# Router logits with the router's weights stationary and the tokens streaming, and an order of steps written for that

## The reference, cut to what matters

```
logits = einsum('th,eh->te', x, gate_weight)      # 512 tokens x 32 experts
probs = softmax(logits)
top_val, top_idx = top_k(probs, 8);  top_val = top_val / sum(top_val)
w_tg = top_val summed into 8 groups by merge_groups[top_idx]
h = einsum('th,goh->tgo', x, gate_up_proj[dominant_experts])
gate, up = split(h);  act = silu(gate) * up
out = einsum('tg,tgh->th', w_tg, einsum('tgi,ghi->tgh', act, down))
```

## Time and profile before

| | us |
|---|---|
| median of three runs | 1121.26 |
| lowest, highest | 1115.88, 1122.84 |
| the profiled execution | 1118.26 |
| its span, first to last instruction | 1116.2 |
| one element in the loop (the copy L906 of one element to that of the next, 302.07 to 432.10) | 130.03 |
| TensorE busy over the span | 1019.5 |
| VectorE busy over the span | 755.6 |
| ScalarE busy over the span | 400.0 |
| GpSimd busy over the span | 420.0 |

### The profile page before, as it was taken

One profiled execution on the slowest core, in us unless ns is written; L12 is line 12 of the kernel. 1 busy time (PEld: TensorE's weight loads), 2 busy tenths in 40 slices (PEclk: granted clock), 3 DMA queues, 4 the chain that ended last, 5 costly groups with the idle time before them and its releaser, 6 DMA issues.

```text
span 1116.2 us, 24959 instructions
## 1 busy us (share of the span) xinstructions
PE 1019.5 (91%) x9856; PEld 739.1 (66%) x9856; DVE 755.6 (68%) x1516; ACT 400.0 (36%) x715; POOL 420.0 (38%) x349
## 2 busy tenths in 40 slices
PE   6979989999999999999899999999999998998768
PEld 4556667766776667766676667766677666776456
DVE  6767677675867767586776858577675777757335
ACT  4335432254214533154322542144331553224210
POOL 1627333364316333273333643154332733326100
PEclk9989999999999999999999999999999999999879
DMA  6220000200011000200002000010002000010000
GB/s 187 57 86 2 1 1 1 68 2 2 1 27 43 2 1 1 68 2 1 1 1 69 1 2 1 10 59 2 2 1 68 2 2 1 1 49 2 2 0 19
DMA packets 22232, 23.59 MB, mean 21 GB/s; under 512 B 6314, under 2 KB 20138, under 8 KB 22130
## 3 DMA queue, kind: packets, MB, share of 16 engines
q1 hardware_dynamic: 22130, 22.02, 6.5%
HBM read 17.80 MB, written 4.21 MB: 20 GB/s over the span
## 4 chain that ended last, share of the span: by engine, by line
PE 82%; DVE 9%; issue 4%; ACT 3%; POOL 1%; DMA 1%; DVEq 0%; POOLq 0%; ACTq 0%; SPq 0%
PE ring L1119 17%; PE ring L976 13%; PE ring L977 10%; PE ring L978 10%; PE ring L1190 8%; PE av L1135 6%; PE ring L1099 6%; DVE mcol L858 3%; PE ring L1090 2%; PE ring L1037 2%; PE ring L1107 1%; PE ring L1179 1%; PE av L1148 1%; ACT pt L670 1%; ACT xn L629 1%
## 5 line engine op out<-in xcount | busy, mean ns | idle before, releaser
L670 ACT ACTIVATE pt<-ring 128x384 f32<-128x384 f32 (+1 forms) x384 | 171.0, 533 | 357.5 <-PE ring L1119 315.0
L858 DVE TENSOR_REDUCE mcol<-ring 128x1 f32<-128x128 f32 (+3 forms) x512 | 212.0, 481 | 51.5 <-PE ring L1099 49.5
L560 POOL TENSOR_SCALAR_AFFINE_SELECT pt<-pt 128x512 f32<-128x512 f32 x128 | 83.2, 662 | 345.2 <-ACT pt L670 345.2
L834 DVE TENSOR_TENSOR prod<-ring,table 128x1024 f32<-128x1024 f32 x128 | 156.2, 1221 | 81.4 <-PE ring L978 59.2
L1119 PE MATMUL ring<-rows 32*128 32x512 f32 (+3 forms) x3072 | 165.2, 329 | 25.9 <-DVE mcol L858 15.7
L551 POOL TENSOR_TENSOR rows<-prod,rows 128x1024 fp32r<-128x1024 f32 x64 | 152.4, 2385 | 86.9 <-ACT rows L650 86.9
L1119 PEld LDWEIGHTS ring<-rows 32*128 32x128 f32 x3072 | 118.9, 185 | 74.8 <-issue 41.3
L544 POOL TENSOR_TENSOR prod<-prod 128x512 f32<-128x512 f32 x64 | 84.7, 1324 | 112.3 <-DVE prod L834 112.1
L976 PE MATMUL ring<-h_hi,gu_lo 128*128 128x512 f32 x192 | 80.7, 420 | 14.2 <-DVE h_lo L819 14.2
L1135 PE MATMUL av<-pt,vals 128*17 128x512 f32 (+3 forms) x1024 | 83.7, 440 | 10.1 <-POOL pt L560 10.1
L976 PE MATMUL ring<-h_hi,wq_lo 128*128 128x512 f32 x192 | 84.1, 438 | 1.8 <-DVE wq_lo L780 1.5
(11 more groups left out here) (159 smaller groups left out, 1651.4 us busy)
## 6 DMA issues: line engine op xcount, KB each, us to landing
xn<-x_dram SPq DMA_DIRECT2D x8, 512.0 KB, 4.3
xr<-x_dram SPq DMA_DIRECT2D x8, 512.0 KB, 3.7
out_dram<-xr SPq DMA_DIRECT2D x8, 512.0 KB, 3.2
gate_bc<-gates_scratch SPq DMA_DIRECT2D x8, 256.0 KB, 5.0
pt<-wmod_dram SPq DMA_DIRECT2D x1, 1536.0 KB, 6.4
pt<-gup_t_dram SPq DMA_DIRECT2D x16, 96.0 KB, 2.6
dn<-wu_t_dram SPq DMA_DIRECT2D x1, 640.0 KB, 9.8
xr<-wk_t_dram SPq DMA_DIRECT2D x1, 512.0 KB, 7.9
```

The costliest lines, as they stand in the source:

```text
L670: sc.activation(pt[:, PT_AT[n] + h * w:PT_AT[n] + (h + 1) * w], ps[:, 0:w], ACT.Exp, scale=SCALE).then_inc(exp_ready.sem, 1)
L834: ve.tensor_tensor(prod[:, s % PROD, :, :], ps[:, :].unsqueeze(1).broadcast_to([P, 2, S]), table[:, :, :], ALU.mult).then_inc(rotated.sem, 1)
L858: last = ve.reduce_max(mcol[:, q, h * HR + HD:h * HR + HD + 1], ps[:, at:at + (q + 1) * P], AX_X)
```

## The change

It does three things. First, the logits are computed with the router's 32 columns of weights as the stationary operand and all 512 tokens streaming, six matmuls, so that the output stands as experts by tokens in 32 partitions of the same ring bank. Second, this has to be turned back: ScalarE copies the 32 partitions to SBUF (`logits_copy`), TensorE transposes four blocks into `av` (`turn_l`), and VectorE copies from there (`turned_l`) in the place of `logits_out`. The values of the next element, which also use `av`, wait for that copy. Third, both texts of the order are written anew; the setup's is as it was. The body's text has 252 steps for 250.

```diff
-                "logits": lambda: (logits_read, ahead, 0),
+                "logits": lambda: (logits_copied, ahead, 0),
...
+                    elif kind == "logits_copy":
+                        ps = wait_full(sc, b, part, ("logits", ahead))
+                        sc.activation(lgT, ps[0:NX, :], ACT.Copy).then_inc(logits_copied.sem, 1)
...
-                    elif kind == "logits_out":
-                        ps = wait_full(ve, b, part, ("logits", ahead))
-                        ve.tensor_copy(lg, ps[:, 0:TT * NX].rearrange("p (t n) -> p t n", t=TT)).then_inc(logits_read.sem, 1)
+                    elif kind == "turned_l":
+                        wait(ve, logits_turned, b, ahead, 0)
+                        ve.tensor_copy(lg, av[:, 0:TT * NX].rearrange("p (t n) -> p t n", t=TT)).then_inc(logits_read.sem, 1)
...
-                                wait(pe, mix_gated, b, ahead - 1, 0)
+                                wait(pe, logits_read, b, ahead - 1, 0)
...
                     elif kind == "logits":
                         ps = take_bank(pe, b, part, step)
+                        three(ps[0:NX, :], *columns(gw_hi, gw_lo, 0, NX), *rows2,
+                              ready=lambda c: wait(pe, lo_ready[1], b, ahead, c)).then_inc(full_sem, 1)
+                    elif kind == "turn_l":
+                        wait_alone(pe, logits_copied, b, ahead, 0)
+                        wait_alone(pe, mix_gated, b, ahead, 0)
                         for t in range(TT):
-                            tok = t * P
-                            last = three(ps[:, t * NX:(t + 1) * NX],
-                                         lambda c: h2_hi[:, c, tok:tok + P], lambda c: h2_lo[:, c, tok:tok + P],
-                                         lambda c: gw_hi[:, c, :], lambda c: gw_lo[:, c, :],
-                                         ready=lambda c: wait(pe, lo_ready[1], b, ahead, c) if t == 0 else None)
-                        last.then_inc(full_sem, 1)
+                            last = pe.transpose(av[:, t * NX:(t + 1) * NX], lgT[:, t * P:(t + 1) * P], ident[0:NX, 0:NX])
+                        last.then_inc(logits_turned.sem, 1)
```

Two lines of the body's text, as an example of the third part (the end of the attention, then the router):

```diff
-combine.101 qcon.10 exp.031 score.032 qcon_hi.10 value.030 qcon_lo.10 hi.101 exp.032 clear.031 lo.100 value.031
+score.031 clear.030 value.030 exp.031 score.032 clear.031 rope.1010 exp.032 clear.032 rope.1011 value.031 value.032
```

More of the change, by code:

```diff
@@ L103 @@
-weighed.00 weighed.01 weigh.04 weigh.05 upped.05 weighed.02 weighed.03 hi.111 weighed.04 weighed.05 down.00 lo.110
-kcon_hi.11 kcon_lo.11 join.00 down.01 join.01 lo.111 store.0
+load_next.1 loads.0 maxima.010 rope.0200 reduce.010 score.000 rotate.0200 rope.0201 exp.000 rotate.0201 maxima.011
+rope.0210 clear.000 reduce.011 score.001 rope.0211 exp.001 rotate.0210 combine.020 clear.001 maxima.012 rotate.0211
+combine.021 value.000 value.001 reduce.012 score.002 hi.020 shift.01 qcon.02 lo.020 exp.002 kcon.02 qcon_hi.02
@@ new lines @@
+modulate1.11 low1.10 score.020 exp.020 score.021 low1.11 clear.020 exp.021 attn_out.01 clear.021 rope.1000
+maxima.031 rotate.1000 value.020 reduce.031 maxima.032 reduce.032 value.021 score.022 exp.022 shift.03 shifted.03
+rope.1001 score.030 clear.022 value.022 rotate.1001 exp.030 attn_out.02 latent.1 latent_hi.1 latent_lo.1 combine.100
+score.031 clear.030 value.030 exp.031 score.032 clear.031 rope.1010 exp.032 clear.032 rope.1011 value.031 value.032
+hi.100 lo.100 rotate.1010 rotate.1011 kcon.10 kcon_hi.10 attn_out.03 values.10 rope.1100 combine.101 hi.101 mix.00
@@ new lines @@
+mix.01 values.11 rotate.1100 kcon_lo.10 qcon.10 mixed.00 mixed.01 values_out.10 qcon_hi.10 lo.101 qcon_lo.10
+maxima.100 stats2.0 reduce.100 values_out.11 maxima.101 rope.1101 rope.1110 pow2.0 norm2.0 turn2.00 reduce.101
+turn2.01 rotate.1101 modulate2.00 rope.1111 modulate2.01 qcon.11 qcon_hi.11 rotate.1110 combine.110 low2.00
+maxima.102 low2.01 logits.0 rotate.1111 logits_copy.0 qcon_lo.11 gate.00 hi.110 combine.111 turn_l.0 lo.110
+reduce.102 turned_l.0 tanh.00 hi.111 gate.01 tanh.01 gate.02 tanh.02 gated.00 up.00 up.01 top.0 shift.10 gate.03
@@ L119 @@
[L119 to L123 removed]
+loads.0 maxima.010 rope.0200 reduce.010 score.000 rotate.0200 rope.0201 exp.000 rotate.0201 maxima.011 rope.0210
@@ new lines @@
+clear.000 reduce.011 score.001 rope.0211 exp.001 rotate.0210 combine.020 clear.001 maxima.012 rotate.0211
+combine.021 value.000 value.001 reduce.012 score.002 hi.020 shift.01 qcon.02 lo.020 exp.002 kcon.02 qcon_hi.02
+clear.002 rope.0300 shifted.01 hi.021 qcon_lo.02 kcon_hi.02 score.010 rotate.0300 value.002 exp.010 rope.0301
+kcon_lo.02 score.011 attn_out.00 lo.021 rope.0310 rotate.0301 exp.011 maxima.020 clear.010 value.010 rotate.0310
+combine.030 reduce.020 score.012 exp.012 rope.0311 maxima.021 qcon.03 rotate.0311 reduce.021 maxima.022 combine.031
```

56 lines of the change are left out of this document (21 added, 35 removed).

## The result

The changed kernel took 1101.43 us in the median of four runs (1100.39 to 1104.50), the kernel before 1119.99 beside it; the ratio is 0.9842, with a 95% interval from 0.9803 to 0.9880. The forecast of 1093 was 8 us too low, and the time lies just beyond the forecast's own range (1084 to 1100); the range for 8 in 10, 1084 to 1110, held it because that takes in the rival *half filled* as well.

What follows compares the result with a forecast made beforehand. TensorE was taken to bound the kernel, busy 1019.5 of 1116.2 us. Net 2.9 us of waits plus 0.6 for the router, 3.5 times 7, plus 1.7 gave 26.2 us less: 1093 us, range for 8 in 10 1084 to 1110.

Steps and rivals of the forecast that it cites:

- half filled: Rival, chance 0.18: the two larger new waits come out twice as long as VectorE's queue slips; 11 us more, 1104.
- The router's work: Router logits on TensorE: 2.68 - 1.40 - 0.36 - 0.3 for changes of form, 0.6 us less per element.
- the two figures cited there: The Trainium skill's matmul prices: about 25 ns start to start for short ones, 215.7 ns for 512 columns.
- The filled waits: Five TensorE waits per loop element, 0.88, 0.62, 1.06, 1.14 and 1.49, filled by the new order: together 5.19 us.
- cover of 2.4 us against 2.2: Ahead of `mix.00`: `kcon.10`, `values.10` and `rope.1100` take 2.4 us on TensorE and cover `attn_out.03`, 2.2 us.
- The new waits: Waits the new order makes: 0.8 at `maxima.030`, 0.8 at `maxima.100`, 0.7 for smaller ones; 2.3 us per element.
- 0.7 together, between 0 and 1.5: Smaller new waits per element: `maxima.101` for a bank of `maxima.100`, and `gate.00` for a bank read by `rotate.1111`.
- The clock: Granted clock in the loop, 1.00 in the profile before; its fall under 1.00 was named only as a sign of error.
- two of the signs named there: Signs of a wrong forecast: an element over 128.5 us, and the loop's granted clock under 1.00.
- The last element: Element without a next one: 2.5 us of waits filled, router 0.6, less 0.8 and 0.6; sum 1.7 us.
- GpSimd's queue: Rival *slower*, chance 0.06: late GpSimd work makes TensorE wait at `value.002` and `value.011`, 5.85 us per element, 1133.
- the covers of 0.8 and 0.4: Slack in us expected before TensorE would wait on GpSimd at `value.002` (0.8) and `value.011` (0.4); cost nothing.

Runs made afterwards that it cites:

- e9: The changed kernel with six matmuls whose result nobody reads put between `maxima.100` and `maxima.101`; 1096.76 us.
- e5: The kernel of e3, but GpSimd's `lo.101` waits for the second residual addition on VectorE instead of the first; 1085.40 us.
- e6: The kernel of e5 with `rope.1101` put ahead of `maxima.101` on TensorE and `rotate.1101` ahead of `reduce.101` on VectorE; 1082.36 us.
- e3: The changed kernel with two GpSimd waits more: `combine.101` until `attn_out.03` has multiplied, `lo.101` until the first residual addition is done; 1089.56 us.
- e12: The order and two GpSimd waits of e6 with the old router of 24 short matmuls; 1099.29 us.
- e1: The changed kernel's new order of steps with the old router of 24 short matmuls; 1118.14 us, ratio 0.9988 to the kernel before.
- e10: The kernel of e1 with six matmuls whose result nobody reads put between `maxima.100` and `maxima.101`; 1120.74 us.
- e2: The kernel before, in its old order of steps, with the new router; 1106.30 us, ratio 0.9888 to the kernel before.
- e8: The kernel of e2 with GpSimd's `lo.100` moved behind `clear.032` and held so that it runs beside the multiplication of `attn_out.03`; 1133.06 us.

## Why the prediction was right, and which step failed

- **The router's work**, 0.6 us per element: 0.75 measured (1.40 for six matmuls, 0.36 for the transposes). The 0.3 for changes of form was too much; the rest of the term held. `turn_l` waits for nothing. (By the two figures cited there the total would be some 16 us above the forecast and not 13, if all terms but these are kept: 0.6 - 1.3 instead of 2.68 - 1.40, times 8.)
- **The filled waits**, 5.19 us: four of the five are gone, 0.88, 0.62, 1.06 and 1.49. The fifth, `mix.00`, is 0.88 where the walk gave none: **this is the first step that failed**, an overlap taken for whole. Its cover of 2.4 us against 2.2 was right for VectorE alone; I had read 2.2 from the earlier trace rows, where GpSimd was idle beside the multiplication, and did not look at what the new order puts there.
- **The new waits.** `maxima.030` comes 1.07 us behind the transposes in front of it, with an idle row of 0.41 in between, where it was 0.50 before: 0.6 for my 0.8. The row names no releaser, so that it is VectorE, as I wrote, isn't shown. `maxima.100` waits 0.87 for my 0.8. `gate.00` waits for nothing. `maxima.101` waits 1.55, twice my price for the two together and just over its upper end. **This is the second step that failed: "0.7 together, between 0 and 1.5".** I counted one reduce for it, and not that VectorE comes to that reduce late: from 402.95 to the reduce at 411.61 it works nearly without a break, and the residual addition in it is 1 us longer than before.
- **The clock** was not a term of the sum at all, only in the last sentence as a sign of being wrong, and the sign came: 0.50 in 413.60:416.30, some 1.0 us in this element, and in four of the seven. **A term put at nothing is the third step that failed.** e9 puts it at 4.7 us in all. By two of the signs named there the forecast itself was wrong: an element of 129.0 us is over 128.5, and the clock fell.
- **The last element**: 4.4 for 1.7. The wait for `low2` ahead of the logits and experts is 2.36 instead of 3.69, since the logits come first and begin on the first chunk; the clock of 0.50 behind the old logits (1082.50:1085.60) is gone. Neither was booked there. That this error of 2.7 us runs against the others is luck: without it the forecast would have been 11 us off.
- **The rivals.** GpSimd's queue did not decide: no idle row stands at `value.002` or `value.011`, the covers of 0.8 and 0.4 held. GpSimd did decide something, but by running beside VectorE and not by being late. "Half filled" gave a time close to the measured one, 1104, but only in part for the reason it named. VectorE does slip; but the two larger new waits, at `maxima.030` and `maxima.100`, did not come out twice as long (0.6 and 0.87), and its "VectorE's work is the same" missed that the same work takes longer.

The sum with what was measured, for the element of 129.00 us: 126.5 forecast, + 0.88 at `mix.00`, + 0.85 at `maxima.101`, + 1.0 of clock, - 0.15 for the router, - 0.2 at `maxima.030`, gives 128.9. With the collision taken away, in e5, six of the seven elements are without a stretch at 0.50 and take 126.5, the forecast element; with `maxima.101` filled too, in e6, they take 125.9. That the terms add up is worked out; that each is real is shown by e3 and e5 (collision), e9 (clock) and e6 (both).

The Trainium skill has the collision: its page "SBUF — State Buffer", section "SBUF: two separate sides", says that VectorE with two SBUF inputs and a GpSimd operation that reads SBUF take a shared port pair for a whole instruction, and the other fully blocks. The runs agree: 0.42 becomes 0.88, 1.50 and 2.38, and each time the end lies 0.28 us behind the end of one GpSimd operation that had started first, L551, L546 and L555. On the clock, the page "TensorE: Matmul & The Clock Gate", section "A second HAM failure mode: psum-queue depth-cycling", says that frequent short idle times between groups of matmuls can make the clock go down and up. The trace agrees with waits of 0.88, 0.87 and 1.55 us, in four of seven elements.

Open is why the old order does not suffer behind its 24 short matmuls: before, the clock fell there once in the profile and in e12 four times. There the logits stand between long matmuls of `gate.00` and `gate.01`, in the new order right behind the narrow ones of `maxima.102`; no run separates this. A wait of 0.2 us for the second chunk, which the 24 have between them in some elements of e1 and e10, isn't what it takes: in e12 there is none. Nor is it shown why in some kernels the clock falls in four of seven like elements and in others in all. Open is also what part of e2's 12.2 us is not the form's 6 and not the stretches seen, for only one execution of each is profiled.

## What to carry to other kernels

When a new order moves an engine's work, look at what will run beside it on GpSimd, and not only at what stands ahead of it: an operation with both operands in SBUF can take several times its price and show no wait. Read the granted clock as a price of order: waits that lie close together can cost a second time in the matmuls behind them (1.0 us behind 3.3 us of waits here), many short matmuls in a row can cost more there than in themselves, and two changes that each treat one such place can be worth more together than the sum of both. And where a chain on another engine sets the pace, move work of one's own into the wait instead of moving the wait.

## What the runs showed of the hardware

- A VectorE multiplication of 256 columns with both operands in SBUF, 0.42 us alone, took 1.50 beside a GpSimd subtraction of 1.30 (the changed kernel) and 2.38 beside one of 2.34 (e8), ending 0.28 behind it both times; a residual addition of 0.69 took 1.64 and 1.49 beside one of 2.4 (the changed kernel, e3), ending 0.55 behind it. An operation with one operand in PSUM kept its 0.69 (L899).
- Three waits of 0.9, 0.9 and 1.5 us within 10 us were followed by a granted clock of 0.50 in four of seven elements; with the last of them filled by matmuls (e9), it stayed at 1.00 in all. A stretch of 3.4 us at 0.50 made an element 1.0 us longer there.
- 24 matmuls of 32 columns, one every 0.11 us, were followed by 0.50 as well, or met it before their end: in the new order, in seven of seven elements of e10 and in four of e12. Six matmuls of 512 columns in their place were not (e9, e6). At 0.50 a matmul of 512 columns costs 0.43 us instead of 0.23.
